# A hybrid state-space and expert layer on one core: the sum over the 16 states by float32 transposes, with a copy and transposes back, and one PSUM bank for the experts

## What is computed

```python
dA = exp(clip(dt[..., None] * A, -10, 0))
h = dA * h + dt[..., None] * bt[:, None, :] * xt[..., None]
# every 16th token: h is scaled down where its norm over the 16 states is above 10
y = einsum('bn,ben->be', ct, h) + D_param * xt      # the sum over the 16 states
y = y * silu(z)
out = y @ out_proj_w.T + out_proj_b
```

## Time and profile before

| | |
|---|---|
| runs | 4411.19, 4413.03, 4411.19 us; median 4411.19 |
| profiled execution | span 4411.3 us, 79580 instructions, mean granted TensorE clock 0.993 |
| TensorE matmuls | 4238.2 us busy (96%) |
| TensorE weight loads, beside them | 2946.0 us (67%) |
| VectorE | 3617.9 us (82%) |
| ScalarE | 3086.4 us (70%) |
| GpSimd | 2589.9 us (59%) |
| costliest groups | expert matmuls L712 1920.8 us; scans L948 1240.8; GpSimd's inputs L362 1204.9 and products L354 1122.1; sums over the states L686 966.9 |

### The profile page before, as it was taken

How to read it: one execution, slowest core, us unless ns; L and a number is a source line. 1 busy time by engine, 2 the same in 40 slices (tenths; PEclk the granted TensorE clock), 3 DMA queues, 4 the chain that set the end, 5 groups by cost and what they waited for, 6 DMA issues and landing times.

```text
span 4411.3 us, 79580 instructions
## 1 busy us (share of the span) xinstructions
PE 4238.2 (96%) x22592; PEld 2946.0 (67%) x22592; DVE 3617.9 (82%) x9566; ACT 3086.4 (70%) x9104; POOL 2589.9 (59%) x1284
## 2 busy tenths in 40 slices
PE   6899999999999999999999999979999999999999
PEld 5777777777777777777777777744445454454454
DVE  4899999999999999999999999974667667666677
ACT  6899999999999999999999999844332433333321
POOL 4998988888888989889888989950000000000000
PEclk8999999999999999999999999999999999999999
DMA  3111111111111111111111111110000000000000
GB/s 113 55 54 56 51 62 50 59 55 59 55 59 53 55 56 50 60 54 59 55 59 55 57 52 55 58 42 22 7 16 7 16 16 7 16 16 8 5 8 10
DMA packets 91560, 187.49 MB, mean 43 GB/s; under 512 B 16160, under 2 KB 58016, under 8 KB 90912
## 3 DMA queue, kind: packets, MB, share of 16 engines
q1 hardware_dynamic: 91424, 185.92, 12.7%
HBM read 168.05 MB, written 17.83 MB: 42 GB/s over the span
## 4 chain that ended last, share of the span: by engine, by line
PE 42%; POOL 21%; issue 19%; DVE 14%; ACT 3%; DVEq 1%; POOLq 1%; SPq 0%; DMA 0%; ACTq 0%
PE ps L712 22%; POOL prod L354 12%; POOL hb L362 6%; PE ps L686 5%; DVE macc L1039 4%; PE ps L842 3%; PE ps L824 2%; POOL u L371 1%; POOL xcv L378 1%; PE ps L782 1%; PE ps L807 1%; DVE dtt L1221 1%; ACT zr L415 1%; PE ps_dA L842 1%; PE ps_dA L824 1%
## 5 line engine op out<-in xcount | busy, mean ns | idle before, releaser
L712 PE MATMUL ps<-w_x,mxT 128*128 128x512 f32 x4096 | 1920.8, 597 | 30.8 <-DVE macc L1039 30.8
L948 DVE TENSOR_TENSOR_SCAN hb<-ps_dA,hb 128x1088 f32<-128x1088 f32 x512 | 1240.8, 2423 | 125.3 <-POOL hb L362 119.2
L1039 DVE SCALAR_TENSOR_TENSOR macc<-ps,gate,macc 128x256 f32<-128x256 f32 x2048 | 978.2, 478 | 443.9 <-PE ps L712 360.7
L354 POOL TENSOR_TENSOR prod<-hb,cbc 128x1024 f32<-128x1024 f32 x512 | 1122.1, 2192 | 217.9 <-DVE hb L967 217.9
L362 POOL TENSOR_TENSOR hb<-u,bbc 128x1024 f32<-128x1024 f32 x512 | 1204.9, 2353 | 75.1 <-POOL prod L354 70.7
L415 ACT ACTIVATE zr<-dt,aneg 128x128 f32<-128x128 f32 x4096 | 1239.7, 387 | 0.0
L712 PEld LDWEIGHTS ps<-w_x,mxT 128*128 128x128 f32 x4096 | 724.1, 191 | 694.8 <-issue 592.0
L686 PEld LDWEIGHTS ps<-prod,ident 128*128 128x128 f32 x8192 | 949.6, 193 | 81.4 <-issue 59.4
L686 PE MATMUL ps<-prod,ident 128*128 128x128 f32 x8192 | 966.9, 277 | 11.1 <-POOL prod L354 8.9
L424 ACT ACTIVATE ps_dA<-zr 128x1024 f32<-128x1024 f32 x512 | 517.9, 1011 | 0.0
L430 ACT ACTIVATE sq<-hb 128x64 f32<-128x64 f32 x512 | 157.8, 308 | 194.9 <-DVE hb L948 194.7
(11 more groups left out here) (194 smaller groups left out, 4814.7 us busy)
## 6 DMA issues: line engine op xcount, KB each, us to landing
bbc<-bcd SPq DMA_DIRECT2D x128, 512.0 KB, 3.7
cbc<-bcd SPq DMA_DIRECT2D x128, 512.0 KB, 3.7
xt<-in_x SPq DMA_DIRECT2D x128, 128.0 KB, 3.6
x2d<-macc SPq DMA_DIRECT2D x64, 128.0 KB, 1.7
out_dram<-macc SPq DMA_DIRECT2D x64, 128.0 KB, 1.7
w_x<-in_w_x SPq DMA_DIRECT2D x1, 4096.0 KB, 15.0
hb<-x2d SPq DMA_DIRECT2D x32, 128.0 KB, 2.3
sz<-x2d SPq DMA_DIRECT2D x16, 128.0 KB, 2.3
```

What stands on the lines that cost most here:

```text
L354: TT(dst, states, cc, ALU.mult).then_inc(M["prodp"], 1)
L712: last = mm(banks[p % len(banks)][:], mxT[k][:, j, :], w_x[:, j, p * 512:(p + 1) * 512], start=(j == 0), stop=(j == KD - 1))
L948: V.tensor_tensor_scan(states, dA, states, 0.0, ALU.mult, ALU.add).then_inc(M["scan"], 1)
L1039: STT(macc[k][:], banks[(e // 2) % len(banks)][:, (e % 2) * D:(e % 2 + 1) * D], gate[k][:, e:e + 1], macc[k][:], ALU.mult, ALU.add).then_i ...
```

## The change

1. `sum_states` now has the product slice as weights and the identity as the moving operand, with `is_transpose`, and adds the 16 transposes up in the bank `YT` (which was G1). The sum then lies there with tokens and blocks of channels on the partitions. The first quarter waits until YT has been copied out.
2. VectorE copies YT to SBUF (`yT`) in one instruction in chunk 1, behind the expert sums, and ahead of the sum of squares.
3. TensorE turns the copy back with four transposes (`sums_back`) that add to YP, on top of the term with `D_param`, as the first work of its chunk 1. VectorE's multiplication by the gate waits for it (`M["yb"]`), and for `M["ldt"]`.
4. The experts have one bank (`GM = (G0,)`) in the steps and for the late pairs, so a pair waits for the sums of the pair just before it. TensorE issues pair c+1 at the end of its chunk c, but in chunk 4 between the convolution and the second half of the input projection. From the first attention stage with a second mixture on, both banks are used as before.
5. `dtt` (the input of the softplus) shares the buffer `sg`, to make room for `yT`.

```diff
-        dtt = sb("dtt", [P, EB, P])
+        dtt = sg
+        yT = sb("yT", [P, E])
...
+        GM, YT = (G0,), G1
...
             def sum_states(i, h):
 
                 products_done(pe, i, (h + 1) * QC - 1)
+                if h == 0:
+                    pe.wait_ge(M["yt"], AHEAD + i)
                 for n in range(N):
-                    last = mm(YP[:, h * P:(h + 1) * P], ident[:],
-                              prod[h % 2][:, n, :, :].rearrange("p e t -> p (e t)"), start=False, stop=(h == 3 and n == N - 1))
+                    last = mm(YT[:, h * P:(h + 1) * P], prod[h % 2][:, n, :, :].rearrange("p e t -> p (e t)"), ident[:],
+                              start=(h == 0 and n == 0), stop=(h == 3 and n == N - 1), is_transpose=True)
                 last.then_inc(M["y"], 1)
+
+            def sums_back(i):
+
+                pe.wait_ge(M["yt"], AHEAD + i + 1)
+                for h in range(4):
+                    last = mm(YP[:, h * P:(h + 1) * P], yT[:, h * P:(h + 1) * P], ident[:], start=False, stop=(h == 3),
+                              is_transpose=True)
+                last.then_inc(M["yb"], 1)
...
+                def pair(c):
+
+                    if c < 7 and Y and in_time(i, c + 1):
+                        experts_mm(i - 3, 1 - k, c + 1, c + 2, GM)
+                    if c == 7 and X_ and not (isinstance(i, int) and i == NTILES + 1):
+                        experts_mm(i - 2, k, 0, 1, GM)
+
                 for c in range(NC):
-                    if c < 7 and Y and in_time(i, c + 1):
-                        experts_mm(i - 3, 1 - k, c + 1, c + 2)
...
                     if c == 1:
+                        if B:
+                            sums_back(i - 1)
...
                         last.then_inc(M["conv"], 1)
+                    if c == 4:
+                        pair(c)
+                    if c == 4 and F:
...
-                    if c == 7:
-                        if X_ and not (isinstance(i, int) and i == NTILES + 1):
-                            experts_mm(i - 2, k, 0, 1)
-                        if S_:
-                            sum_states(i, 2)
+                    if c == 7 and S_:
+                        sum_states(i, 2)
+                    if c != 4:
+                        pair(c)
...
-                    experts_mm(m, m % 2, q, q + 1)
+                    experts_mm(m, m % 2, q, q + 1, GM)
                 if b > 0:
-                    experts_mm(n + NTILES, n % 2, p, p + 1, G4 if b == NB else G, fresh=(b == NB and t == 0))
+                    experts_mm(n + NTILES, n % 2, p, p + 1, G4 if b == NB else G, fresh=(b in (1, NB) and t == 0))
...
-                        expert_sums(i - 3, 1 - k, 2 * c, 2 * c + 2)
+                        expert_sums(i - 3, 1 - k, 2 * c, 2 * c + 2, GM)
...
                 start(1)
+                if B:
+                    v.wait_ge(M["y"], AHEAD + i * 4)
+                    V.tensor_copy(yT[:], YT[:]).then_inc(M["yt"], 1)
                 halfway(1)
                 if B:
-                    v.wait_ge(M["y"], AHEAD + i * 4)
+                    v.wait_ge(M["yb"], AHEAD + i)
+                    v.wait_ge(M["ldt"], AHEAD + (i + 2 if G_ else NTILES))
```

More of the change, by code:

```diff
@@ L159, in build @@
         dve_m = ("st1", "mv1", "vp", "den", "sx1", "nx", "keep", "xib", "zb", "xcc", "bcv", "dtb", "scan", "nr",
-                 "st0", "hs", "yg", "o1", "o2", "st3", "mv3", "vc3", "se3", "r3", "o3", "o4")
+                 "st0", "hs", "yg", "o1", "o2", "yt", "st3", "mv3", "vc3", "se3", "r3", "o3", "o4")
         act_m = ("xn", "carry", "lnp", "r1", "qs", "xnTs", "ez", "lz", "ss", "ex", "lx", "sx", "edt", "ldt", "zr", "dA", "sq", "nl",
@@ L163, in build @@
         pool_m = ("sz", "xcv", "u", "bt", "prodp", "x1")
-        pe_m = ("xnT", "xi", "z", "conv", "bc", "dtp", "y", "op")
+        pe_m = ("xnT", "xi", "z", "conv", "bc", "dtp", "y", "yb", "op")
         sp_m = ("x", "xr", "bcd", "bb0", "bb1", "cc0", "cc1")
@@ L701, in logits, with experts_mm @@
                 last.then_inc(R["lg"], 1)
-            def experts_mm(n, k, lo, hi, banks=G, fresh=False):
+            def experts_mm(n, k, lo, hi, banks, fresh=False):
                 for p in range(lo, hi):
@@ L1031, in route_gate, with expert_sums @@
                 TS(gate[k][:], selp[:], ms[:, 11:12], None, ALU.mult).then_inc(R["router"], 1)
-            def expert_sums(n, k, lo, hi, banks=G):
+            def expert_sums(n, k, lo, hi, banks):
                 if lo == 0:
@@ L1343, in slot @@
                     m, q = late_pair(t * (X // 2) + p)
-                    expert_sums(m, m % 2, 2 * q, 2 * q + 2)
+                    expert_sums(m, m % 2, 2 * q, 2 * q + 2, GM)
                 if b > 0:
```

## The result

The changed kernel takes 4667.01 us (4663.07 to 4670.90) against 4411.19: the ratio is 1.0579, 95% interval 1.0564 to 1.0594. I had forecast 4548 and a range up to 4650; it is slower by 256 us, not 137. The direction and the reasons in chunks 1 and 2 held; over half of the loss, 136 us, came from a place that the prediction did not look at.

A forecast was written before the change was run, and what follows sets the result against it. The prediction took the loop of waits between VectorE and GpSimd as the bound, with TensorE beside it. 62 x (1.0 + 1.2) = 136, + 5 - 4 = 137 us on 4411.3 gave 4548 us, range 4430 to 4650.

The forecast's parts named there:

- TensorE is not the bound: Steady tile: VectorE and GpSimd's loop sets the period, so 7.7 us less of TensorE's work on the sums buys nothing.
- The round trip, 1.0 us per tile: Chunk 1: copy and transposes back delay the output projection, so chunk 3's scan comes 1.0 us later (0.7 to 1.1).
- The clock, 1.2 us per tile: TensorE's 3.6 us gap in chunk 1 halves its clock for later work, costing 1.2 us per tile (0 to 1.7).
- One bank, +5 us, 0 to 10: Late expert pairs under the first attention stage wait for VectorE's sums four to five times: +5 us once; steady tiles pay nothing.
- The shorter sums in the drain, -4 us: In the drain the shorter sums over the states lie on the end's path once or twice, saving 4 us.
- The change, part by part: The prediction's section pricing sums, round trip, expert bank, TensorE's clock, aliases and ends; forecast 4548 us in all.
- the sum, 62 x (1.0 + 1.2) + 5 - 4: 62 tiles in the loop pay round trip and clock, plus one bank, minus the drain: 137 us more.
- the likeliest case: Whole kernel: round trip and clock loss both paid, 4548 us, own range 4505 to 4590; chance 0.46.
- Rival 2: Transposes leave TensorE's clock low before the projection's block: 1.7 to 3 us lost per tile, 4580 to 4660 us; chance 0.15.

The follow-up runs named there:

- e1: Changed kernel with 120 empty semaphore increments in VectorE's queue ahead of its loop; 4531.20 us.
- e4: e1 with TensorE's chunk 1 reordered: input projection and router's transposes before the transposes back, not behind them; 4442.31 us.
- e6: Kernel before with only the sums over the states as transposes: no copy, no way back, two expert banks, result not used; 4420.72 us.
- e11: Kernel before with the last two operations of the output's norm moved from VectorE's chunk 3 to chunks 5 and 6; 4461.21 us.
- e5: Kernel before with only the single expert bank and the expert pairs' new places; 4439.56 us.
- e13: Kernel before with 128 empty increments ahead of VectorE's loop; 4415.12 us.
- e2: Kernel before with 12 empty increments ahead of VectorE's loop; 4535.53 us.
- e12: Kernel before with 140 empty increments ahead of VectorE's loop; 4539.48 us.
- e8: e4 with the projection's bias added by ScalarE instead of VectorE, and two banks for the last eight late pairs; 4566.18 us.
- e9: e8 with 140 instead of 120 empty increments ahead of VectorE's loop; 4572.30 us.
- e7: Kernel before with VectorE's addition of the projection's bias moved from chunk 3 to the end of chunk 2; 4409.98 us.

## Why the prediction was wrong

The 256 us, by steps of one edit each: 136 us are the place of VectorE's code (changed kernel to e1), 89 us the round trip's place in TensorE's queue (e1 to e4), 31 us the rest (e4 to before), of which one bank at the end is 23 to 27. What the code's place costs includes the gaps that the stall tears into TensorE's work: of the 2.5 us that it adds to a tile, 1.8 lie in chunks 7 and 0, and 0.7 in chunks 1 and 2.

- **"TensorE is not the bound."** Right, and the main point: e6 takes 5.3 us of TensorE's busy time out of a tile (forecast were 7.7; part of what is left runs at half clock) and gains nothing. How close behind it is, e11 shows.
- **The round trip, 1.0 us per tile.** Right. In e1's tiles at full clock chunks 1 and 2 take 1.0 us more; the copy was 0.68 us (taken as 0.65), the wait for the projection came last, as worked out, and GpSimd's slack at chunk 3 was used up.
- **The clock, 1.2 us per tile.** In the changed kernel chunks 1 and 2 together grew by 2.16 us, 2.2 forecast. But that was luck. Without the code stall the same gap costs 0.5 us, since the clock falls in it in 13 of 56 tiles, not in 8 of 10: in 22 tiles it fell earlier, in the idle stretch ahead of the last sums, which I had not priced. The work behind it is then slow, the gap before the way back becomes shorter, and the clock is up again when the projection needs it: none of those 22 tiles has a second fall. With the stall, 33 of 56 tiles have the later fall.
- **One bank, +5 us, 0 to 10.** Mis-sized: 23 to 27 us (e5). I counted four or five waits in the attention slots, where the changed kernel has seven, 7.9 us together, and not the pairs of the steps behind the last scan, which now queue behind VectorE there too.
- **The shorter sums in the drain, -4 us.** About right: in e6 the stretch from the last scan to the attention stage takes 106.7 us instead of 109.8.
- **The failed step: "The change, part by part" priced each instruction by what it does, and not where it puts the code behind it; the sum, 62 x (1.0 + 1.2) + 5 - 4, has no term for that, and gives no reason why it should be nothing.** It was 136 us. The added instructions of the steps that are written out ahead of the loop moved VectorE's loop by 7 to 11 entries. It no longer lay where it stays loaded, and behind each backward branch it paid 3.3 to 5.2 us, 99 us as waits of the first scan alone, and 136 with what follows on TensorE. The profile before held the hint, though not the price: the instruction queues had 80 and 56 packets and none of them between 400 and 2756 us, so the loops stayed loaded, and nothing says by how much.
- **Terms that offset one another.** Without the stall e1 is 120 us over the kernel before, where the sum had 137, and its tile of 46.48 us lies in the forecast 46 to 47.5. That too is partly chance: the steady tiles gave 84 us of it and not 136, the end 27 and not 1. The upper bound of the likeliest case, 4590, is by its own terms (2.7 us per tile) 4580.
- **Rival 2 (the transposes leave the clock low).** Not decided as a rule, and not needed for the size: in e4, with 68 transposes in a tile, the mean clock is 0.98 over the steady stretch, in e6, with 64, 0.97. So transposes don't keep the clock down throughout. The Trainium skill's part "PE-mode transpose" on "TensorE: Matmul & The Clock Gate" is neither confirmed nor refuted; no run separates what a transpose counts from the idle time that it leaves.
- **What stays open:** why the range of places that fit is as wide as it is (the queue's first entries aren't all in the trace, so the exact boundary isn't known), whether the unit is 128 or a part of it, and how the remaining 4 to 8 us of the 31 divide (3.3 of them lie in the steady tiles of e4).

## What to carry to other kernels

Where a hardware loop is long, its place in memory is part of the design: look at the packets of the instruction queues, and if an edit raises them, shift the loop by empty instructions before judging the edit. Relief for an engine is worth nothing until the loop of waits runs through it, even where it is busy nearly all of a tile, as TensorE is in the earlier trace rows; an early or late tile with less of its work in it shows that for free. Such an engine can still be the next bound, as e11 shows. A round trip between two engines costs by what stands in the queue between its legs: put the work that must be done anyway into the wait, and not behind it.

## What the runs showed of the hardware

**The place of a loop's code.** VectorE's loop of 369 or 373 entries ran without reloading where it lies in the kernel before, 128 places on from there (e13), and in the changed kernel with 120 empty instructions (e1). It paid about 4 us per round in the changed kernel itself, 12 and 140 places on from the old place (e2, e12), and in e8 and e9. All of it fits one rule, which is inferred and whose boundary was not measured: packets of 8192 bytes, 128 instructions, and a loop that has to lie within three of them (369 and 373 entries are 2.9 packets, so that only 16 or 12 of 128 places fit). The Trainium skill, "Advanced Engine Details and Errata", section "ISA Cache", gives two lines of 256 instructions for engines other than TensorE, as a size that can be configured; with a shift of 140, at which two such lines would hold the loop again, it was loaded in each round, so the measurement decides for the smaller piece. By the Trainium skill, "Runtime: NRT & Kernel Launch", section "Instruction fetch mechanics", a taken branch to a place that is not loaded forces a fetch before execution goes on; the 4.60 us of "issue" with an instruction packet in them agree.

**VectorE beside GpSimd.** An operation of VectorE with two operands in SBUF (L1157, L1160) that began beside one of GpSimd's ended only behind it: 0.49 us became 0.87 (median in e7) to 1.33 (mean in e11), and in e11 L1186 ended 0.28 us behind GpSimd's in 62 of 64 tiles, whenever it had begun. The scans and the expert sums, which read PSUM, kept their 2.42 and 0.48 us. The Trainium skill, "SBUF — State Buffer", section "SBUF: two separate sides", describes an exclusive lock on the port pair that the two engines share; the rows agree. This is why these two operations gave no gain when they were moved: they met GpSimd in both new places, and what chunk 3 gave back was lost to TensorE in chunk 4.
